# Scaling the attention probabilities on GpSimd instead of VectorE in a four-layer fused kernel

## The reference

```
q, k, v = proj(wq), proj(wk), proj(wv)          # 32 heads of 16
q, k = _apply_rope(q, sin, cos), _apply_rope(k, sin, cos)
scores = einsum('bnth,bnsh->bnts', q, k) / sqrt(16)
scores = where(causal, scores, -inf)
attn = softmax(scores, axis=-1)
out = einsum('bnts,bnsh->bnth', attn, v)        # then times wo, added to x
```

## Time and profile before

| | |
|---|---|
| Median of 3 runs | 1597.06 us (1591.18 to 1598.67) |
| The profiled execution | 1588.73 us, span 1586.9 us |
| Busy share of the span | TensorE 90%, VectorE 71%, ScalarE 46%, GpSimd 27% |
| First attention's turns | from 51.7 us to some 355 us of the span |
| VectorE busy from 51 to 350 us | 222.8 us of 299 |
| TensorE busy from 51 to 350 us | 248.9 us of 299 |
| GpSimd busy from 51 to 350 us | 23.7 us of 299 |
| Mean granted TensorE clock from 51 to 350 us | 0.99 of full speed |

### The profile page before, as it was taken

The page is one execution under the profiler, slowest core; times in us unless marked ns, Lnnn a source line. Parts: engine busy times, 40 slices in busy tenths (PEclk is TensorE's granted clock), DMA queues, the critical chain, the costliest instruction groups (busy, mean ns, idle before and its releaser), DMA issues.

```text
span 1586.9 us, 26588 instructions
## 1 busy us (share of the span) xinstructions
PE 1430.3 (90%) x9332; PEld 1215.0 (77%) x9332; DVE 1120.2 (71%) x2171; ACT 735.7 (46%) x1996; POOL 432.0 (27%) x328
## 2 busy tenths in 40 slices
PE   4888888869999797899999999999999999958998
PEld 3776767547777585788888988889888988846887
DVE  6686868678999853546776778767687767863554
ACT  3675757532222221425555555555555555532332
POOL 5100000003223370433343241434243342315000
PEclk9999999999999999699999999999999999988999
DMA  6000010113322000210202010020202120010000
GB/s 198 28 1 28 1 57 10 40 41 102 118 79 73 7 14 2 74 34 28 67 28 67 26 33 33 26 66 26 66 26 66 26 66 14 13 47 20 15 13 26
DMA packets 39681, 67.80 MB, mean 43 GB/s; under 512 B 4940, under 2 KB 13799, under 8 KB 39618
## 3 DMA queue, kind: packets, MB, share of 16 engines
q1 hardware_dynamic: 37522, 65.69, 13.2%
q10 hardware_dynamic: 2096, 1.30, 0.3%
HBM read 60.65 MB, written 2.13 MB: 40 GB/s over the span
## 4 chain that ended last, share of the span: by engine, by line
PE 59%; DVE 21%; issue 13%; POOL 3%; ACT 3%; DMA 1%; SPq 0%; POOLq 0%; DVEq 0%; ACTq 0%
PE PS L325 14%; PE PS L327 14%; PE PS L326 14%; DVE E_p L1253 3%; DVE A_mx L1024 2%; DVE E_nb L1244 2%; DVE E_mx L1240 2%; PE PS L1793 2%; DVE A_pT L1011 2%; DVE E_T L1262 1%; PE PS L1776 1%; PE PS L1459 1%; PE PS L1491 1%; POOL E_sw L526 1%; PE PS L1480 1%
## 5 line engine op out<-in xcount | busy, mean ns | idle before, releaser
L325 PE MATMUL PS<-XNH,E_WL 128*128 128x256 f32 x768 | 218.1, 284 | 6.7 <-POOL E_WL L440 5.9
L326 PE MATMUL PS<-XNL,E_WH 128*128 128x256 f32 x768 | 214.4, 279 | 0.0
L327 PE MATMUL PS<-XNH,E_WH 128*128 128x256 f32 x768 | 214.2, 279 | 0.0
L526 POOL TENSOR_TENSOR E_sw<-E_sw,rope2s 128x1024 f32<-128x1024 f32 x64 | 103.3, 1615 | 309.9 <-ACT E_sw L578 309.9
L1240 DVE TENSOR_REDUCE E_mx<-PS 128x4 f32<-128x512 f32 x64 | 60.8, 951 | 139.2 <-PE PS L1779 139.2
L325 PEld LDWEIGHTS PS<-XNH,E_WL 128*128 128x128 f32 x768 | 144.7, 188 | 11.1 <-POOL E_WL L440 8.9
L326 PEld LDWEIGHTS PS<-XNL,E_WH 128*128 128x128 f32 x768 | 144.5, 188 | 1.0
L327 PEld LDWEIGHTS PS<-XNH,E_WH 128*128 128x128 f32 x768 | 144.4, 188 | 0.0
L791 ACT ACTIVATE E_p<-PS,E_nb 128x128 f32<-128x128 f32 (+1 forms) x256 | 103.8, 431 | 85.1 <-DVE E_nb L1244 85.1
L578 ACT ACTIVATE E_sw<-PS 64x256 f32<-64x256 f32 (+1 forms) x128 | 89.5, 699 | 103.8 <-PE PS L327 102.3
L440 POOL TENSOR_TENSOR E_WL<-raw,E_WH 128x512 fp32r<-128x512 f32 x80 | 102.7, 1319 | 124.6 <-ACT E_WH L578 124.6
(11 more groups left out here) (266 smaller groups left out, 4260.3 us busy)
## 6 DMA issues: line engine op xcount, KB each, us to landing
raw<-in_w SPq DMA_DIRECT2D x104, 256.0 KB, 2.9
words<-in_words SPq DMA_DIRECT2D x11, 768.0 KB, 4.3
wo<-in_wo SPq DMA_DIRECT2D x32, 256.0 KB, 3.9
zb<-z_scratch SPq DMA_DIRECT2D x11, 384.0 KB, 5.1
scb<-in_scales SPq DMA_DIRECT2D x11, 384.0 KB, 5.6
X<-in_x SPq DMA_DIRECT2D x8, 256.0 KB, 5.7
SGH<-XNH SPq DMA_DIRECT2D x8, 256.0 KB, 2.7
SGL<-XNL SPq DMA_DIRECT2D x8, 256.0 KB, 2.9
```

Source lines behind the costliest of these rows:

```text
L325: nc.tensor.matmul(o, sl, mh, start=first, stop=False)
L326: nc.tensor.matmul(o, sh, ml, start=False, stop=False)
L327: return nc.tensor.matmul(o, sh, mh, start=False, stop=last)
L526: nc.gpsimd.tensor_tensor(E_sw[:, heads, :], E_sw[:, heads, :], rope2s[:, :].unsqueeze(1).broadcast_to([P, heads.stop - heads.start, SEQ]) ...
```

## The change

The eight `tensor_scalar` a turn on VectorE go. GpSimd gets the function `weigh`: one `tensor_tensor` for each query block, which multiplies all four heads' blocks in place (128 x 512 for `tb` = 0, 128 x 1024 for `tb` = 1) by the reciprocals, repeated along the keys. It waits for `rec` and signals `pn`. In the turn's order on GpSimd the first comes before `sines`, the second after it. VectorE keeps the reciprocals; before each it waits for the `pn` of the turn before. The three products of `scale_tile(0, 0)` are issued by GpSimd in turns 3, 4 and 5 of the last batch, one in each, and no longer after it.

```diff
+            def weigh(b, g, tb):
+
+                t, wide = b * G0 + g, (tb + 1) * P
+                pool.wait_ge(a["rec"], t * 2 + (tb + 1))
+                blocks = A_ps[g % 2][:, 0:4, :] if tb == 0 else A_ps[g % 2][:, 4:12, :].rearrange("p (n s) t -> p n (s t)", s=2)
+                nc.gpsimd.tensor_tensor(blocks, blocks, A_rec[:, 4 * tb:4 * tb + 4].unsqueeze(2).broadcast_to([P, 4, wide]), ALU.mult)\
+                  .then_inc(a["pn"], 1)
+
             def attend(b):
                 for g in range(G0):
                     unit = prepared(b, g)
+                    weigh(b, g, 0)
                     if unit:
                         sines(unit[0], unit[3])
+                    weigh(b, g, 1)
+                    if isinstance(b, int) and b == NB - 1 and 3 <= g < 6:
+                        scale_tile(0, 0, (g - 3,))
...
-            scale_tile(0, 0)
             finish(pool, 2)
...
                     for tb in range(2):
                         dve.wait_ge(a["exp"], t * 2 + (tb + 1))
+                        after(dve, a["pn"], t * 2 + (tb - 1))
                         V.reciprocal(A_rec[:, 4 * tb:4 * tb + 4], A_sum[:, 4 * tb:4 * tb + 4]).then_inc(a["rec"], 1)
-                        dve.wait_ge(a["rec"], t * 2 + (tb + 1))
-                        for n in range(4):
-                            blocks = slice(n, n + 1) if tb == 0 else slice(4 + 2 * n, 6 + 2 * n)
-                            ins = V.tensor_scalar(A_ps[g % 2][:, blocks, :], A_ps[g % 2][:, blocks, :], A_rec[:, 4 * tb + n:4 * tb + n + 1], None, ALU.mult)
-                        ins.then_inc(a["pn"], 1)
```

More of the change, by code:

```diff
@@ L462, in attend, with scale_tile @@
                     unit = prepared(b, g)
+                    weigh(b, g, 0)
                     if unit:
                         sines(unit[0], unit[3])
+                    weigh(b, g, 1)
+                    if isinstance(b, int) and b == NB - 1 and 3 <= g < 6:
+                        scale_tile(0, 0, (g - 3,))
+            def scale_tile(n, p, weights=(0, 1, 2)):
+                for c in weights:
+                    pool.wait_ge(f["t"], n * 3 + (c + 1))
+                    if not isinstance(n, int) or n >= 1:
+                        pool.wait_ge(f["lo"], n * 3 + (c - 2))
+                    nc.gpsimd.tensor_tensor(F_w[:, c, :], F_t[:, c, :], scb[p][:, c, :], ALU.mult).then_inc(f["w"], 1)
             for g in FIRST:
```

## The result

| | before | after |
|---|---|---|
| Median | 1594.55 us (1591.18 to 1598.67, 4 runs) | 1613.05 us (1610.14 to 1615.3, 4 runs) |
| Ratio | | 1.0114, 95% interval 1.0079 to 1.0149 |
| Profiled execution, span | 1588.73 us, 1586.9 us | 1611.03 us, 1609.2 us |

The kernel became slower by 1.1%. The forecast was 1617 us with a range of 1607 to 1627.

What follows compares the result with a forecast made beforehand. The bound was taken to be the first attention's per-turn chain through VectorE, ScalarE and TensorE, without the moved multiplications. Ten pure turns (+16.7 us) and the last five (+3.4) gave +20.1: 1608.8 profiled, 1617 on the median, range 1607 to 1627.

Steps and rivals of the forecast that it cites:

- (a): First attention: VectorE loses 2.02 us of multiplications a turn; worth nothing in 27 turns with a unit, something in the last five.
- (b): GpSimd gains two products a turn: the small one hides before the sine product, the large one takes 1.89 us.
- rival 1: Large GpSimd product takes 2.39 us, by L526's row: +28.7 us, 1626; chance 0.16.
- (c): Large product holds VectorE's rotation: pure turns (no value projection or output product) 9.17 us for 7.50; ten give +16.7 us.
- (d): Last five turns, no rotation: product holds other VectorE work; +0.5 us in four, +1.4 in the last, together +3.4.
- its clock part: Near relative of rival 1: TensorE's granted clock falls earlier in the last turns, +1 us a turn, up to +5.
- Rival 2: Rotation gets the SBUF inputs before the large product, which then holds the next turn's L1028: +14.4 us, 1611; chance 0.09.
- Rival 3: GpSimd's product with the repeated operand doesn't hold VectorE: sum +1 us, 1598, no change; chance 0.09.

Runs made afterwards that it cites:

- e8_no_scaling: Kernel before with VectorE's multiplications by the reciprocals left out and nothing in their place (output not the reference's): 1590.38 us, ratio 0.9975 to the kernel before.
- e2_unused_product: Kernel before plus one 128x1024 GpSimd product behind each sine product, its result never read or waited for: 1610.35 us, ratio 1.0089 to the kernel before.
- e3_rotation_from_psum: Changed kernel with the cosine product written to PSUM, so the rotation has one SBUF input: 1605.24 us, ratio 1.0062 to the kernel before.
- e4_two_halves: Changed kernel with the 128x1024 product issued as two of 128x512: 1603.77 us, ratio 1.0048 to the kernel before.
- e6_both_behind_sines: Changed kernel with both GpSimd products behind the sine product, the small one first: 1617.11 us, ratio 1.0139 to the kernel before.
- e7_last_turns_only: Changed kernel with GpSimd scaling only in the last five turns, VectorE multiplying in the 27 others: 1596.06 us, ratio 1.0010 to the kernel before.
- e5_small_product_only: Changed kernel with only tb = 0 scaled on GpSimd, tb = 1 back on VectorE: 1593.23 us, ratio 0.9993 to the kernel before.

## Why the prediction was right

(a) What bounds: the chain of the earlier trace rows left the multiplications out, and e8_no_scaling confirms it: pure turns don't move without them. In the last five turns, where the prediction had the multiplications on the chain throughout, it shows them to count in g = 4 and not in g = 3.

(b) The large product was put at 1.89 us from L501's operand form and measures 1.89 to 1.90 in most places; the small one 1.04. L526's row of 2.39 would have been wrong, and so would the Trainium skill's 2.6 cycles an element (GPSIMD Engine Reference, Elementwise side-by-side cycle accounting): (1.895 - 1.04)/512 = 1.67 ns an element is 2.0 cycles at 1.2 GHz. With an operand repeated along the innermost dimension the measurement is below the page's figure, and decides. The 3 to 5 us that the prediction adds by that figure are for the ten pure turns alone; for a product of such a length rival 1 has 8.6 in all.

(c) The hold: the rotation was put at +7.16 to +9.26 and a pure turn at 9.17. Turn g = 3 of batch 2 starts at 244.49; measured from there the product runs from +7.03 to +8.92, the rotation from +7.16 to +9.20, and the turn is 9.13 long. The rotation ends 0.28 us after the product, as worked out from L973. Ten turns at 1.60 give 16.0 for the forecast 16.7. e2_unused_product shows the mechanism without any dependence, e3_rotation_from_psum which operands it needs, e4_two_halves and e6_both_behind_sines how the turn passes from one engine to the other. The Trainium skill's rule of an exclusive lock for the whole instruction (SBUF — State Buffer, SBUF: two separate sides) agrees with them: the rotation with two SBUF inputs is held for the whole product (2.04 us), and in e4_two_halves the second half waits in its turn. The section says nothing of the reciprocal by name; here it isn't held (0.18), and neither is a copy out of PSUM (L1051, 0.42 us at 339.85, beside a product from 339.58 to 341.48).

(d) The last five turns: +3.4 forecast, +2.7 in the profiled execution (1.6, 0.3, 0.4, 0.0, 0.4), +1.6 by the timed runs of e7_last_turns_only. The sum is near, its parts are not, so that is luck: g = 3 grew by 1.6 and not 0.5, at a granted clock of 0.81 in the turn, and e5_small_product_only has the same 8.90 us there without a large product. The last turn was put at +1.4 and came to +0.4: I had taken its late second reciprocal (+5.3) as given, but it came from ScalarE waiting for TensorE at low clock, and now comes at +4.5.

The forecast 1617 stands against 1613.05. On the profiled execution it was 1608.8 against 1611.03: +19.4 in the attention for the +20.1 of the sum, and +2.9 outside, which the sum didn't have. The median of before was itself 1597.06 over three runs and 1594.66 over 26 later, so some 2.4 us of the difference of 4 is that.

Rival 1 (a product of 2.39 us) falls with (b); its clock part is seen, 1.6 us in g = 3 where it had +1 a turn and up to +5. Rival 2 (the rotation first) didn't occur in any turn: GpSimd's next instruction starts with the end of the sine product, 0.13 us before the rotation. Rival 3 (no hold) falls with L1008's 2.04 us.

## What to carry to other kernels

Before work goes from VectorE to GpSimd, look at what VectorE does in the stretch where the GpSimd instruction will run: here instructions with two SBUF inputs, and scalar ones from SBUF to SBUF, that came up behind it stood still until it ended. A rotation of 0.43 us at the head of the queue cost each pure turn 1.6 us, and the 2.02 us of work that were moved had cost it nothing. Where it must be moved, order GpSimd's queue so that the long instruction runs while VectorE reads PSUM (here three quarters of the pure turns' loss back by swapping two lines), or split it (half of it back). And ask first, by leaving the work out, whether the engine to be relieved bounds at all.

## What the runs showed of the hardware

- The hold depends on operands: a rotation of 128x256 takes 2.04 us with both inputs in SBUF and 0.42 with one in PSUM, beside the same product. Row maxima out of PSUM (0.68), a copy out of PSUM (0.42) and reciprocals (0.17 to 0.18) take no longer beside a product than without one.
- A held instruction ends 0.28 us after the product (work of 0.43), 0.54 (work of 0.69) or 0.02 (a bias of 0.17): each time its own length less 0.15.
- Between two GpSimd instructions without a gap, a waiting VectorE instruction gets in, and the second GpSimd instruction then waits: two halves of 1.04 us take 2.22.
- GpSimd's product with a second operand repeated along the innermost dimension costs 1.67 ns an element. With one that is repeated over the heads only, and steps along the innermost dimension, it is 2.15 by L457 and L526 of the earlier trace rows.
- The granted clock of TensorE is 1.00 in most of the attention and lower in some turns, which are longer for it: g = 3 of the last batch takes 7.27 to 7.40 us at 1.00 and 8.85 to 8.90 at 0.81, whatever the kernel. After the change TensorE was busy 3.10 of 5 us where it began to fall (0.87 in 60 to 65, then 0.79) and 2.75 of 5 before the 0.67 of 330 to 335; but 2.60 of 5 in 350 to 355 were followed by 1.00. The lowest is 0.50, in 58 to 64 us with both products behind the sine product. Which turns it meets differs between kernels and no run here tells why, so single turns of single executions shouldn't be compared without their clock.
